# Last stage of a graph network kernel: rows copied into a ring by step before TensorE sums them

## What is computed

```python
all_msg = jnp.einsum('nf,rfo->rno', h, weight)            # 16 relations
msg = all_msg[rel_type, src] * norm
gate = jax.nn.sigmoid(all_gate[rel_type, src])[:, None]
msg = msg * gate
agg = jax.ops.segment_sum(msg, dst, num_segments=n_nodes)
return jax.nn.relu(agg)                                   # added to x
```

## Time and profile before

| | us |
|---|---|
| median of 3 runs | 5541.65 |
| lowest and highest run | 5539.95, 5544.51 |
| span of the profiled execution, first to last instruction | 6401.9 |
| gathers of the last stage in it, first to last start | 4052.6 to 6375.6 |

### The profile page before, as it was taken

The page is one execution under the profiler, slowest core; times in us unless marked ns, Lnnn a source line. Parts: engine busy times, 40 slices in busy tenths (PEclk is TensorE's granted clock), DMA queues, the critical chain, the costliest instruction groups (busy, mean ns, idle before and its releaser), DMA issues. The chain is left out here.

```text
span 6401.9 us, 106223 instructions
## 1 busy us (share of the span) xinstructions
PE 4687.5 (73%) x21476; PEld 2770.0 (43%) x21477; DVE 3466.9 (54%) x7990; ACT 3306.9 (52%) x8030; POOL 3423.4 (53%) x3416
## 2 busy tenths in 40 slices
PE   8788888888888888888789999545554445555555
PEld 5345445454444544445444444233333333333333
DVE  6487778888877887878853333222222222222224
ACT  3477777777777777777544444333333333333332
POOL 0366666666666666666610000466666666666665
PEclk9899999999999999999899999766666666666666
DMA  4466666766666666666644444333333333333334
GB/s 138 148 193 192 189 190 193 198 192 193 186 192 186 196 190 193 190 190 197 185 137 140 141 140 140 111 89 89 89 88 89 89 89 87 90 88 87 89 89 116
DMA packets 551965, 929.49 MB, mean 145 GB/s; under 512 B 112845, under 2 KB 361823, under 8 KB 551904
## 3 DMA queue, kind: packets, MB, share of 16 engines
q0 software_dynamic: 208384, 648.75, 36.3%
q1 hardware_dynamic: 343520, 280.03, 13.7%
HBM read 795.60 MB, written 132.88 MB: 145 GB/s over the span
## 5 line engine op out<-in xcount | busy, mean ns | idle before, releaser
L1006 POOL DMA_INDIRECT kv_rows<-kv_d,idx x1664 | 1751.9, 1053 | 1138.4 <-PE sums L1200 593.1
L1786 PE MATMUL m_sums<-m_rows,m_oh 128*128 x3328 | 1176.7, 512 | 1165.0 <-issue 908.6
L1723 POOL DMA_INDIRECT m_rows<-msg_d,m_idx x1568 | 1499.2, 956 | 854.8 <-issue 464.6
L1766 ACT ACTIVATE m_rows<-m_rows,m_norm 128x256 f32<-128x256 f32 x1568 | 710.8, 500 | 1628.9 <-DMA m_rows<-msg_d,m_idx 1528.2
L1786 PEld LDWEIGHTS m_sums<-m_rows,m_oh 128*128 128x128 f32 x3328 | 800.0, 256 | 1542.1 <-issue 1422.7
L1808 DVE TENSOR_TENSOR agg<-agg,m_sums 128x256 f32 x832 | 349.3, 420 | 1673.7 <-DMA kv_rows<-kv_d,idx 1005.8
L1200 PE MATMUL sums<-kv_rows,onehot 128*128 128x264 f32 x3328 | 984.3, 420 | 47.4 <-ACT onehot L1077 18.5
L1040 ACT ACTIVATE hid<-p_hid,b1s 128x512 f32<-128x512 f32 x784 | 495.6, 683 | 648.0 <-remote 226.9
L1200 PEld LDWEIGHTS sums<-kv_rows,onehot 128*128 128x128 f32 x3328 | 590.0, 197 | 461.8 <-issue 346.0
L1157 PE MATMUL p_q<-shelf,pickT 128*128 x4992 | 718.3, 281 | 56.8 <-ACT pickT L1063 28.2
L1656 PE MATMUL p_m<-wr,h1T 128*128 128x512 f32 x1568 | 710.1, 596 | 0.0
(11 more groups left out here) (194 smaller groups left out, 4459.9 us busy)
## 6 DMA issues: line engine op xcount, KB each, us to landing
msg_d<-msg SPq DMA_DIRECT2D x196, 512.0 KB, 2.9
dsts<-dstrow_d SPq DMA_DIRECT2D x208, 256.0 KB
ef_raw<-in_edge_attr_dram SPq DMA_DIRECT2D x195, 256.0 KB
kv_rows<-kv_d,idx POOLq DMA_INDIRECT x1664
m_rows<-msg_d,m_idx POOLq DMA_INDIRECT x1568
kv_d<-kvo SPq DMA_DIRECT2D x49, 260.0 KB, 2.1
pens<-pens_d SPq DMA_DIRECT2D x104, 96.2 KB
emlp<-mlp_d SPq DMA_DIRECT2D x104, 64.0 KB
```

Source lines behind the costliest of these rows:

```text
L1006: pool.indirect_dma_start(rows[:, u, k, :], None, kv_d[:, :], bass.IndirectOffsetOnAxis(idx[:, half, c:c + 1], 0)).then_inc(gathered[u], 16)
L1723: pool.indirect_dma_start(rows[:, u, k, :], None, msg_d[:, :], bass.IndirectOffsetOnAxis(idx[:, u // HALF, c:c + 1], 0)).then_inc(gathered ...
L1766: last = nc.scalar.activation(rows[:, u, k, :], rows[:, u, k, :], ACT.Copy, scale=norm[:, bass.ds(2 * g + k, 1)])
L1786: last = nc.tensor.matmul(sums[u % BANKS][:, 0:D], onehot[:, u % HOTS, k, :], rows[:, bass.ds(slot, 1), k, :].rearrange("p a d -> p (a d)" ...
```

## The change

ScalarE no longer weighs in place by group. It works by step: it loads the group numbers of four steps, waits for the one-hot matrix, for the bank's sum and for the group's arrival, and writes the weighed rows of the step from their slot into a new ring `step_rows` of 8 entries. TensorE reads `step_rows` at fixed addresses, loads no registers, and waits once for two steps. A slot of `rows` is free once ScalarE's copies have passed the steps of its group; GpSimd loads `past` itself and waits for `weighed`. SyncE now waits for each group's arrival in order and counts it as `arrived`; after 8 groups it loads the next half of `idx`.

```diff
+        step_rows = sb("m_step_rows", [P, BANKS, 2, D])
...
+        arrived = sem("m_arrived")
-        freed = sem("m_freed")
...
@@ gpsimd
-                    if u % 2 == 0 and not (isinstance(i, int) and i == 0):
-                        hold(pool, freed, HALF * i + u // 2 + 1 - HALF, pool_go)
+                    if not (isinstance(i, int) and i == 0):
+                        if u % LOADS == 0:
+                            done = load_four(nc, pool, past, RING * i + u - RING, 1, STEPS)
+                        if u % 2 == 0:
+                            hold(pool, weighed, done[u % LOADS + 1] & 1023, pool_go)
...
@@ sync
-                for last in (1, 3):
-                    hold(sp, summed, done[last] & 1023, freed)
...
+            def load(i, v):
+                sp.dma_start(idx[:, v, :], rel_d[:, bass.ds(2 * (RING * i + HALF * v), 2 * HALF)]).then_inc(idx_in[v], 16)
+
+            def body(i, more):
+                full = 32 * (i + 1) if isinstance(i, int) else sp.snap(32 * (i + 1))
+                for u in range(RING):
+                    hold(sp, gathered[u], full, arrived)
+                    if more and u % HALF == HALF - 1:
+                        load(i + 1, u // HALF)
...
@@ scalar
-                    g = RING * i + u
-                    act.wait_ge(gathered[u], 32 * (i + 1))
+                    s = RING * i + u
+                    if u % LOADS == 0:
+                        four = load_four(nc, act, t["groups"], s, 1, GROUPS)
+                    groups = four[u % LOADS]
+                    act.wait_ge(onehot_ready, s + 1)
+                    if not (isinstance(i, int) and i == 0 and u < BANKS):
+                        act.wait_ge(added, s + 1 - BANKS)
+                    act.wait_ge(arrived, groups & 1023)
+                    slot = act.snap((groups + RING - 1) & (RING - 1))
                     for k in range(2):
-                        last = nc.scalar.activation(rows[:, u, k, :], rows[:, u, k, :], ACT.Copy, scale=norm[:, bass.ds(2 * g + k, 1)])
+                        last = nc.scalar.activation(step_rows[:, u % BANKS, k, :],
+                                                    rows[:, bass.ds(slot, 1), k, :].rearrange("p a d -> p (a d)"),
+                                                    ACT.Copy, scale=norm[:, bass.ds(2 * groups + (k - 2), 1)])
...
@@ tensor
-                    if u % LOADS == 0:
-                        four = load_four(nc, pe, t["groups"], s, 1, GROUPS)
-                    groups = four[u % LOADS]
-                    pe.wait_ge(onehot_ready, s + 1)
-                    pe.wait_ge(weighed, groups & 1023)
-                    if not (isinstance(i, int) and i == 0 and u < BANKS):
-                        pe.wait_ge(added, s + 1 - BANKS)
-                    slot = pe.snap((groups + RING - 1) & (RING - 1))
+                    if u % 2 == 0:
+                        pe.wait_ge(weighed, s + 2)
                     for k in range(2):
-                        last = nc.tensor.matmul(sums[u % BANKS][:, 0:D], onehot[:, u % HOTS, k, :],
-                                                rows[:, bass.ds(slot, 1), k, :].rearrange("p a d -> p (a d)"),
+                        last = nc.tensor.matmul(sums[u % BANKS][:, 0:D], onehot[:, u % HOTS, k, :], step_rows[:, u % BANKS, k, :],
```

More of the change, by code:

```diff
@@ L1724, in body @@
                                                 bass.IndirectOffsetOnAxis(idx[:, u // HALF, c:c + 1], 0)).then_inc(gathered[u], 16)
-            turns(pool, body, GTURNS)
+            body(0)
+            pool.wait_ge(past_in, 16)
+            with pool.Fori(1, GTURNS) as i:
+                body(i)
         @block.sync
         def _(sp):
-            def free(done):
-                for last in (1, 3):
-                    hold(sp, summed, done[last] & 1023, freed)
[L1735 to L1752, removed]
+            def load(i, v):
[6 more added lines that the diff above has]
+                        load(i + 1, u // HALF)
+            load(0, 0)
+            load(0, 1)
+            sp.dma_start(norm[:, :], norm_d).then_inc(norm_in, 16)
+            sp.dma_start(past[:, :], past_d).then_inc(past_in, 16)
+            body(0, True)
+            with sp.Fori(1, GTURNS - 1) as i:
+                body(i, True)
+            body(GTURNS - 1, False)
             for b in range(BLOCKS):
@@ L1762, in body @@
                 for u in range(RING):
-                    g = RING * i + u
-                    act.wait_ge(gathered[u], 32 * (i + 1))
+                    s = RING * i + u
[7 more added lines that the diff above has]
+                    slot = act.snap((groups + RING - 1) & (RING - 1))
                     for k in range(2):
-                        last = nc.scalar.activation(rows[:, u, k, :], rows[:, u, k, :], ACT.Copy, scale=norm[:, bass.ds(2 * g + k, 1)])
+                        last = nc.scalar.activation(step_rows[:, u % BANKS, k, :],
+                                                    rows[:, bass.ds(slot, 1), k, :].rearrange("p a d -> p (a d)"),
+                                                    ACT.Copy, scale=norm[:, bass.ds(2 * groups + (k - 2), 1)])
                     last.then_inc(weighed, 1)
             act.wait_ge(norm_in, 16)
-            turns(act, body, GTURNS)
+            turns(act, body, TURNS)
         @block.tensor
```

## The result

The changed kernel takes 5568.01 us (median of 4 runs, 5564.15 to 5570.39) against 5542.63 us: 25.4 us more, ratio 1.0043 with a 95% interval of 1.0029 to 1.0057. The prediction was 5541 us, no change, with 0.25 for slower by over 0.2%.

A forecast was written before the change was run, and what follows sets the result against it. The prediction took the timed last stage to be bound by POOL's own gathers, end to end. Every part of the change was priced at 0, less or more a microsecond or two at the end: 5541 us, range 5410 to 5620.

The forecast's parts named there:

- What bounds the stage: Last stage, timed runs: bound by POOL's own gathers end to end, 1568 at 0.946 us, 1483 us.
- The sum that led there: 5541.65 less 4052.6 us before the first gather and 26.3 us at the end: 1463 us, 0.933 us a gather.
- the 860 us: Profiled span over median: mostly 0.30 us behind each gather (465 us) and POOL's waits for slots (358 us), together 823 us.
- rival A: Last stage: PE's slow sequencer partly real, so the change removes POOL's slot waits; 5460 or 5358 us; chance 0.27.
- PE crawl: Profiled last stage only: PE's register operations reach 1.4 us, so slots come free late and POOL stops.
- Out of PE, slots free earlier: PE's loads and waits removed, POOL waiting for ScalarE's copy: gain 0 timed, the slots worth 358 us in the profile.
- Onto ACT: ScalarE working by step: 44 us more activation time against 1629 us idle; taken as 0, 98 us over POOL if serial.
- Onto POOL: 192 register loads on GpSimd: taken as 0, hidden; 65 us if uncovered without drain, upper bound 219 us.
- rival B: POOL's register loads are not covered: 5607 us, up to 5760 if each drains POOL; chance 0.13.
- C: Rival: ACT becomes the bound from 1.78 us a step; 5640 us at 1.90; chance 0.07.
- SP: "Cost 0": SyncE: 192 register loads and the frees go, 784 arrival waits come, index loads start no later; cost 0.
- PE runs up to a step later, which counts once, at the end: PE waiting on ScalarE's copies in pairs: up to a step's delay, a microsecond or two at the end.

The follow-up runs named there:

- e6_fewer_gathers: The kernel before without the second gather of every second group from the second turn on, 384 of 1568 left out: 5067.15 us against 5541.65.
- base: The kernel before, unchanged, run once more for a second trace: 5545.51 us in one run, span 5543.6 us.
- e4_pe_each_step: The changed kernel with 38 output stores issued by ScalarE and TensorE waiting for ScalarE's copy before every step: 5544.02 us, ratio 1.0002 to the kernel before.
- e3_pool_frees: The kernel before, but GpSimd loads the table of passed steps itself and waits for TensorE's count, SyncE's frees gone: 5544.36 us, ratio 1.0004.
- e1_stores_late: The kernel before, but SyncE waits for the last group's arrival before issuing the first output store: 5559.60 us, ratio 1.0038.
- e2_act_stores: The changed kernel with 38 of the 49 output stores issued by ScalarE, 11 kept on SyncE: 5551.76 us, ratio 1.0019 to the kernel before.

## Why the prediction was wrong

- *What bounds the stage*: right in name, and proved by `e6_fewer_gathers`. Its price was wrong. I took 0.946 us a gather and gave the 0.30 us behind it to the profile; a gather costs 1.25 us in the timed runs.
- *The sum that led there* failed. It assumed that the stretches ahead of the last stage took as long as in the trace (4052.6 us), and got 0.933 us a gather, below the shortest duration. That impossible figure should have been the warning: the first gather really starts at 3559.5 us. Of the two terms of the 860 us, POOL's waits for slots (358) were right: the last stage's gathers take 354 us less in `base`. The 0.30 us behind each gather (465) was wrong; in its place stand the 494 us by which the attention stage had been stretched, and 11 us at the end. That is also more than the 407 us that rival A called the most that could be missing there. Right by luck was the conclusion that the timed runs have no PE crawl and no wait for slots.
- *The rule of the Trainium skill* that I set aside ("Runtime: NRT & Kernel Launch", The ~15µs preamble/postamble breakdown) has the profile's total some 6.2 us above the time. The second trace agrees with it only in that the two lie close: its span of 5543.6 us is 1.9 us under the time, 5545.51. A span 860 us over the time meant that this execution was another one than the timed ones, not that a trace adds that much.
- *Out of PE, slots free earlier*: 0 and 0, as forecast for the timed runs. The span near 6044 that I derived for the profile from the crawl's waits was not seen (5562.4), because the crawl was not there.
- *Onto ACT*: 0, right. The busy time is 749.6 us against 710.8 (39 more, forecast 44), with 1234 us of idle left. `e4_pe_each_step` has all of it and costs nothing.
- *Onto POOL*: 0, right. 192 loads at 0.325 us, all hidden; rival B falls with `e3_pool_frees`, C with ScalarE's idle time, A with the second profile of the kernel before, in which POOL waits 4.9 us for slots.
- *SP: "Cost 0"*: the step that failed. I priced the loads, frees and waits, and forgot what stands behind them in SyncE's queue: the 49 output stores. The old relay ended a turn early, the new one ends with the last group. `e1_stores_late` puts 17.4 us on it; 18.9 us by the start of the last store.
- *"PE runs up to a step later, which counts once, at the end"*: the second one. The wait for pairs changed when TensorE and VectorE work, and the engine that is the bound paid for it: 75 gathers over 0.97 us in `e2_act_stores` against 37 in `e4_pe_each_step`, 6.6 us of busy time and 7.2 us of the timed runs, all through the stage and not once at the end.

Added up: 17.4 + 7.2 = 24.6 us of the 25.4 measured. That it comes so near is partly luck, since the first term alone is uncertain by several us. The measured time lies in the stated range, but the range leaned to a gain that could not be had, and the slower side was given to mechanisms that did not occur. With both defects mended the change is worth nothing, as its main argument said: `e4_pe_each_step` is 2.4 us from the kernel before, within its interval. No version here beats the kernel before.

## What to carry over

When waits of an engine's queue are moved, look at what stands behind them after the loop, above all at final stores: a relay that ends one turn early leaves room to drain them, one that follows the last arrival puts them all at the end. Where an engine is saturated, a coarser wait on another engine need not be free: here it bunched the work around the saturated one and cost some 7 us of 5542. And when a profiled span is far from the timed runs, check a stage that nobody disputes, or take a second trace, before any wait in it is explained.

## What was not expected of the hardware

- An indirect DMA of 128 rows of 1 KB costs GpSimd 0.946 us (median) and a further 0.30 us in which it starts no other, whichever the kernel; leaving 384 out gave 1.24 us each.
- Issuing a store of 128 KB from SyncE takes 0.49 us from one to the next (49 in 24.06 us in the changed kernel), though the data of nearly all of them is long ready.
- In one profiled execution PE's and SP's register operations reached 1.4 us and two stages were stretched, 860 us in all; in the second trace of the same kernel they stay at 32 to 46 ns in the last stage. What disturbed the first is open.
- Gathers last about 0.1 to 0.2 us longer now and then: 36 to 42 of 1568 over 0.97 us with TensorE waiting step by step, 75 to 81 with pairs, and 88 of 1184 in `e6_fewer_gathers`. Every one of the 349 that start 0.10 to 0.25 us behind the start of a one-hot build of VectorE is among them, and none of 583 that start as far behind an add alone.
